# Two PSUM banks as one tile: paired exponentials and maxima, masks of two-head diagonal tiles on TensorE

## What is computed

```
h = layernorm(x) * (1 + ca) + sa
q, k, v = split(h @ w_in.T)                       # 16 heads of 16
scores = (q @ k.T) * 16 ** -0.5
scores = where(key > query, -inf, scores)         # causal
attn = softmax(scores)                            # row maximum, exp, sum
x = x + ga * ((attn @ v) @ w_out.T + b_out)
h = layernorm(x) * (1 + cb) + sb
x = x + gb * (sigmoid(xr @ W_r) * (relu(xk @ W_k) ** 2 @ W_v))   # xr, xk: h mixed with the token before
```

## Time and profile before

| | us |
|---|---|
| median of 3 runs | 1524.66 (1518.13 to 1531.08) |
| the profiled execution | 1521.95 |
| its span, first to last instruction | 1520.0 |

### The profile page before, as it was taken

The page is one execution under the profiler, slowest core; times in us unless marked ns, Lnnn a source line. Parts: engine busy times, 40 slices in busy tenths (PEclk is TensorE's granted clock), DMA queues, the critical chain, the costliest instruction groups (busy, mean ns, idle before and its releaser), DMA issues.

```text
span 1520.0 us, 28003 instructions
## 1 busy us (share of the span) xinstructions
PE 1346.2 (89%) x8744; PEld 746.3 (49%) x8744; DVE 1118.0 (74%) x3435; ACT 958.2 (63%) x1916; POOL 678.7 (45%) x1098
## 2 busy tenths in 40 slices
PE   5898889899998999889998899989998999998855
PEld 4443434455554555444554455545454555544444
DVE  8778667877678777877678777787778777777234
ACT  2167556766677666676677566776667666666633
POOL 4014122554436354553446545364546534343554
PEclk9598979999899999999899999999999898999878
DMA  4321124122331224222242223312232222221100
GB/s 139 75 64 47 42 50 112 49 65 68 84 86 46 54 66 118 67 54 55 67 108 53 56 70 97 82 44 54 72 105 63 64 54 76 68 58 50 38 29 28
DMA packets 90005, 101.77 MB, mean 67 GB/s; under 512 B 29681, under 2 KB 55545, under 8 KB 89857
## 3 DMA queue, kind: packets, MB, share of 16 engines
q1 hardware_dynamic: 89280, 99.20, 25.0%
q10 hardware_dynamic: 576, 0.79, 0.3%
HBM read 30.69 MB, written 8.94 MB: 26 GB/s over the span
## 4 chain that ended last, share of the span: by engine, by line
PE 51%; DVE 13%; SPq 10%; ACT 9%; issue 8%; POOL 7%; DMA 2%; ACTq 0%; POOLq 0%; DVEq 0%
PE val_ps L1286 13%; PE col_ps L1235 12%; PE row_ps L1264 9%; SPq L493 6%; ACT weights L815 5%; DVE row_ps L1035 5%; PE dense_ps L1296 4%; SPq L505 3%; PE dense_ps L1298 3%; PE dense_ps L1297 3%; PE dense_ps L1324 2%; DVE max_parts L1039 2%; POOL weights L664 2%; PE dense_ps L1339 2%; ACT xn_c L859 1%
## 5 line engine op out<-in xcount | busy, mean ns | idle before, releaser
L815 ACT ACTIVATE weights<-col_ps 128x512 f32<-128x512 f32 (+2 forms) x1280 | 643.7, 557 | 319.9 <-PE col_ps L1235 305.2
L1035 DVE CUSTOM_DVE_ANT_0 row_ps<-row_ps,row_mask 128x128 f32<-128x128 f32 (+3 forms) x1024 | 477.4, 517 | 209.7 <-PE row_ps L1264 209.3
L1235 PE MATMUL col_ps<-q_stack,k_stack 64*128 64x512 f32 (+3 forms) x1536 | 400.9, 410 | 36.1 <-ACT weights L815 20.4
L664 POOL TENSOR_SCALAR_AFFINE_SELECT weights<-weights 128x256 f32<-128x256 f32 x512 | 211.0, 425 | 460.1 <-ACT weights L815 458.7
L1039 DVE TENSOR_REDUCE max_parts<-row_ps 128x1 f32<-128x512 f32 x512 | 328.7, 681 | 86.5 <-PE row_ps L1264 84.8
L1286 PE MATMUL val_ps<-weights,v_ones 128*32 128x512 f32 (+3 forms) x3072 | 349.9, 529 | 25.6 <-POOL weights L664 18.1
L1264 PE MATMUL row_ps<-k_stack,q_stack 62*128 62x512 f32 (+3 forms) x1536 | 341.6, 434 | 29.3 <-DVE max_parts L1039 11.8
L1235 PEld LDWEIGHTS col_ps<-q_stack,k_stack 64*128 64x128 f32 x1536 | 210.5, 196 | 224.7 <-ACT weights L815 174.4
L1264 PEld LDWEIGHTS row_ps<-k_stack,q_stack 62*128 62x128 f32 x1536 | 163.8, 197 | 242.2 <-DVE max_parts L1035 79.9
L1035 DVE DVE_READ_ACCUMULATOR2_ANT max_parts<- 128x1 f32 x1024 | 144.7, 141 | 0.0
L1286 PEld LDWEIGHTS val_ps<-weights,v_ones 128*32 128x32 f32 x3072 | 62.1, 110 | 117.8 <-issue 61.6
(11 more groups left out here) (194 smaller groups left out, 1893.8 us busy)
## 6 DMA issues: line engine op xcount, KB each, us to landing
q_stack<-q_part SPq DMA_DIRECT2D x384, 64.0 KB, 2.2
k_stack<-k_part SPq DMA_DIRECT2D x372, 64.0 KB, 2.2
xa<-in_x SPq DMA_DIRECT2D x8, 1024.0 KB, 5.6
q_stack<-max_rows SPq DMA_DIRECT2D x512, 2.0 KB
att<-val_out SPq DMA_DIRECT2D x64, 128.0 KB
recips<-recip_rows SPq DMA_DIRECT2D x32, 256.0 KB
xq<-in_x SPq DMA_DIRECT2D x28, 256.0 KB, 3.3
out<-xq SPq DMA_DIRECT2D x28, 256.0 KB, 2.1
```

The source lines that it names most:

```text
L664: nc.gpsimd.affine_select(out=w, in_=w, compare_op=ALU.is_ge, fill=0.0, base=0, pattern=[[0, 2], [1, P]], channel_multiplier=-1).then_inc( ...
L815: nc.scalar.activation(weights[:, t % 2, heads[0]:heads[-1] + 1:2, 0:q1 - q0], col_ps[bank][:, 0:n * (q1 - q0)].rearrange("p (h q) -> p h ...
L1035: last = nc.vector.tensor_tensor_reduce(out=scores, in0=scores, in1=row_mask[:, HALF - width:HALF], scale=1.0, scalar=MASKED, op0=ALU.add, ...
L1235: last = nc.tensor.matmul(col_ps[bank][:, i * (q1 - q0):(i + 1) * (q1 - q0)], stack_at(k_stack[s % 2], rows, heads[i], P * j, P * (j + 1)) ...
```

## The change

- `col_ps` becomes one tile over both banks (`col_pair`), and `row_ps` two tiles of two banks each. One ScalarE instruction takes the exponentials of both banks of a pair and releases both at its end (`exp_done` rises by 2). 1280 instructions of one bank become 640 of two.
- One `reduce_max` takes the maxima of both banks of a pair.
- The mask of a diagonal unit with two heads a bank (128 or 256 keys) no longer is VectorE's: TensorE adds it in the bank, with eight small bf16 matmuls a pair (`mask_ident` times `mask_fill`, 128 columns and then 64), ahead of the semaphore that VectorE waits for. Units with one head a bank (384 or 512 keys) keep VectorE's custom instruction, two a pair.
- VectorE takes both early maxima of a step before it empties the dense bank; in the code before, one maximum stood before and one behind.
- The maxima are transposed by four 32 by 32 instructions in place of one of 128 by 32, into rows of 128, so that `place_max` needs two DMAs in place of eight.
- GpSimd builds the two mask constants at the start.

```diff
-PLACED = 2 * (P // SQUARE) * 16
+PLACED = 2 * 16
-        col_ps = [ps(f"col_ps{i}", [P, HALF]) for i in range(COL_BANKS)]
-        row_ps = [ps(f"row_ps{i}", [P, HALF]) for i in range(ROW_BANKS)]
+        col_pair = ps("col_ps", [P, COL_BANKS, HALF])
+        row_pair_ps = [ps(f"row_ps{i}", [P, 2, HALF]) for i in range(ROW_BANKS // 2)]
+        col_ps = [col_pair[:, i, :] for i in range(COL_BANKS)]
+        row_ps = [row_pair_ps[i // 2][:, i % 2, :] for i in range(ROW_BANKS)]
...
@@ place_max, SP
-                    for q in range(P // SQUARE):
-                        lo = SQUARE * q + 8 * MROWS * odd
-                        sp.dma_start(rows[:, :, q, :], max_rows[half][lo:lo + 8 * MROWS, :]
-                                     ).then_inc(max_placed[half], 16)
+                    sp.dma_start(stack[row:row + MROWS, half].rearrange("p g n -> p (g n)").bitcast(F32),
+                                 max_rows[half][8 * MROWS * odd:8 * MROWS * (odd + 1), :]).then_inc(max_placed[half], 16)
...
@@ exps, ACT
-                act.wait_ge(cols_ready, exp_index(b, s, c) + 1)
+                act.wait_ge(cols_ready, exp_index(b, s, c) + 2)
-                nc.scalar.activation(weights[:, t % 2, heads[0]:heads[-1] + 1:2, 0:q1 - q0],
-                                     col_ps[bank][:, 0:n * (q1 - q0)].rearrange("p (h q) -> p h q", h=n),
-                                     ACT.Exp, scale=SCALE).then_inc(exp_done, 1)
+                nc.scalar.activation(weights[:, t % 2, heads[0]:heads[0] + 2 * n, 0:q1 - q0].rearrange(
+                    "p (n o) q -> p o n q", o=2), col_pair[:, :, 0:n * (q1 - q0)].rearrange(
+                    "p o (n q) -> p o n q", n=n), ACT.Exp, scale=SCALE).then_inc(exp_done, 2)
...
@@ maximum, DVE
-                dve.wait_ge(rows_ready, at + 1)
+                dve.wait_ge(rows_ready, at + 2)
-                if k1 == P * (i + 1):
+                if k1 == P * (i + 1) and n == 1:
-                    for n in range(len(heads)):
-                        scores = bank[:, n * width:(n + 1) * width]
+                    for o in range(2):
+                        scores = banks[:, o, 0:k1 - k0]
...
-                    last = nc.vector.reduce_max(dest, bank[:, 0:len(heads) * width].rearrange(
-                        "p (h k) -> p h k", h=len(heads)), AX_X)
-                last.then_inc(max_done, 1)
+                    last = nc.vector.reduce_max(dest, banks[:, :, 0:n * (k1 - k0)].rearrange(
+                        "p o (n k) -> p o n k", n=n), AX_X)
+                last.then_inc(max_done, 2)
...
@@ split_max, DVE
-                nc.vector.transpose(max_rows[half][:], parts[:, 0:SQUARE].bitcast(F32)).then_inc(max_turned, 1)
+                for q in range(P // SQUARE):
+                    cols = slice(SQUARE * q, SQUARE * (q + 1))
+                    last = nc.vector.transpose(max_rows[half][:, cols], parts[cols, 0:SQUARE].bitcast(F32))
+                last.then_inc(max_turned, 1)
...
@@ body, DVE
                     for item in at:
                         empty_dense(*item)
-                    for u in early[1:]:
-                        maximum(b, s, u)
                     for item in at:
                         mix(*item)
-                    for u in late:
+                    for u in late[::2]:
                         maximum(b, s, u)
...
@@ row_pair, PE
+                diagonal = k1 == P * (i + 1) and len(pair[0]) == 2
-                        end = n == len(heads) - 1
+                        end = n == len(heads) - 1 and not diagonal
...
+                for n in range(len(pair[0])) if diagonal else ():
+                    for a in range(2):
+                        for odd in range(2):
+                            rows = slice(ROW_TILE * odd, ROW_TILE * (odd + 1))
+                            end = n == len(pair[0]) - 1 and a == 1
+                            last = nc.tensor.matmul(banks[odd][:, (n + 1) * width - P + ROW_TILE * a:(n + 1) * width],
+                                                    mask_ident[rows, a, :], mask_fill[rows, a, ROW_TILE * a:P],
+                                                    start=False, stop=end, skip_group_check=True)
+                            if end:
+                                last.then_inc(rows_ready, 1)
```

More of the change, by code:

```diff
@@ L160, in build @@
         max_parts = [sb(f"max_parts{i}", [P, P], F32R) for i in range(2)]
-        max_rows = [sb(f"max_rows{i}", [P, 2 * MROWS * 8]) for i in range(2)]
+        max_rows = [sb(f"max_rows{i}", [SQUARE, P]) for i in range(2)]
         val_out = [sb(f"val_out{i}", [P, HALF]) for i in range(2)]
@@ L919, in body @@
                     units = range(COL_FIRST[t], COL_FIRST[t + 1]) if attends(kind) else ()
-                    for c in units[:2]:
+                    for c in units[:1]:
                         exps(b, s, t, c)
@@ L924, in body @@
                     normalise_next(b, kind, s, t)
-                    for c in units[2:]:
+                    for c in units[2::2]:
                         exps(b, s, t, c)
@@ L1023, in maximum @@
                 at = unit_index(b, s, u)
-                bank = row_ps[bank_of(UNITS * ((s + 1) % G) + u, UNITS * G, ROW_BANKS)[0]]
-                dve.wait_ge(rows_ready, at + 1)
+                banks = row_pair_ps[bank_of(UNITS * ((s + 1) % G) + u, UNITS * G, ROW_BANKS)[0] // 2]
+                dve.wait_ge(rows_ready, at + 2)
                 i, heads, k0, k1, second = ROW_UNITS[u]
-                half, odd = i // 4, heads[0] % 2
-                col = (SPANS_AT + 16 * second + 8 * odd if half else WHOLE_AT + 16 * odd) + 4 * (heads[0] // 2) + i % 4
@@ L1029, in maximum @@
-                dest = max_parts[half][:, col:col + 4 * len(heads) - 3:4].bitcast(F32)
-                width = k1 - k0
-                if k1 == P * (i + 1):
-                    for n in range(len(heads)):
-                        scores = bank[:, n * width:(n + 1) * width]
+                half, n = i // 4, len(heads)
+                apart = 8 if half else 16
+                col = (SPANS_AT + 16 * second if half else WHOLE_AT) + 4 * (heads[0] // 2) + i % 4
+                dest = max_parts[half][:, col:col + 2 * apart].bitcast(F32).rearrange(
+                    "p (o c) -> p o c", o=2)[:, :, 0:4 * n - 3:4]
@@ L1041, in maximum @@
-                last.then_inc(max_done, 1)
[L1042 to L1045, removed]
+                            out=scores, in0=scores, in1=row_mask[:, HALF - (k1 - k0):HALF], scale=1.0, scalar=MASKED,
+                            op0=ALU.add, op1=ALU.max, accum_out=dest[:, o, :])
+                else:
+                    last = nc.vector.reduce_max(dest, banks[:, :, 0:n * (k1 - k0)].rearrange(
+                        "p o (n k) -> p o n k", n=n), AX_X)
@@ L1047, in split_max @@
+                last.then_inc(max_done, 2)
+                if u == FIRST_HALF - 2:
+                    split_max(b, s, 0, at + 2)
+                if u == UNITS - 2:
+                    split_max(b, s, 1, at + 2)
             def split_max(b, s, half, upto):
```

20 lines of the change are left out of this document (13 added, 7 removed).

## The result

The changed kernel takes 1578.72 us in the median of four executions (1563.33 to 1582.93), the kernel before 1522.78; the ratio is 1.034 (95% interval 1.026 to 1.043), so about 52 us are lost by the ratio and 56 by the medians. The profiled execution took 1575.01 us. The change is slower, as forecast, and by more than the 31 us forecast.

The account below looks back on a forecast made before the run. The prediction saw four loops through TensorE, the one from scores to exponentials tightest. Terms of 94 us lost less 62 gained made +32 us on 1522, near 1553 us; range 1488 to 1608, the forecast's own 1540 to 1580.

Parts of the forecast that it names:

- The paired exponentials: Column banks released together: ScalarE stands until both are refilled, values at t = 0 come 0.38 us later; +29 us.
- 29 + 11 - 10: Column banks released together +29 us, GpSimd's masks starting later +11, shorter exponentials where ScalarE is behind -10.
- The rival of serial banks: Column loop bounds every step of 384 or 512 columns; 93 us paid in place of 29, 1610 us; chance 0.12.
- GpSimd's masks: On the four one-pair steps GpSimd's first mask waits for the whole exponential: +11 us, bounds 0 and 45.
- Masks on TensorE: Eight matmuls for each of 128 diagonal pairs, 0.40 us a pair, 96 pairs counted: +38 us, bounds 18 and 72.
- VectorE: VectorE's work falls by a net 117 to 158 us; TensorE waits less for maxima: -34 us, bounds 0 and -80.
- SP: Two DMAs for eight land maxima 3.9 us earlier: -18 us; three more transposes on the same stretch: +8 us.
- The order: At t = 2 the dense bank is emptied behind a second custom maximum: +8 us, bounds 0 and 24.
- The signs: Observations named beforehand as showing the forecast right (exponential times, gap, VectorE busy, mask times, DMA waits) or wrong.
- Faster: Rival: VectorE is the hidden bound, its relief brings 25 us more and masks cost 18 us; 1490 us, chance 0.25.
- Nothing moves: Rival: TensorE's masks lie in waits that exist anyway and the terms cancel; 1522 us within 15, chance 0.18.

Follow-up runs that it names:

- e1: Changed kernel with exponentials taken and freed one bank at a time again, against the kernel before: 0.994, 1518 us.
- e2: Kernel before with only the paired exponentials added, one instruction over both banks: 1.026 of the kernel before, 1567 us.
- e10: Kernel before with its single-bank exponentials kept, but both banks freed only after the second: 1.018 of the kernel before, 1556 us.
- e11: Kernel before with paired exponentials only at the one-pair steps t = 2, 3, 10 and 11: 1.004 of the kernel before, 1532 us.
- e6: Changed kernel with the mask matmuls on TensorE left out, against the kernel before: 1.026, 1568 us.
- e9: Kernel before with paired maxima and the new order, all masks still on VectorE: 0.999 of the kernel before, 1527 us.
- e7: Changed kernel with exponentials by bank, one transpose and eight DMAs, against the kernel before: 0.993, 1519 us.
- e4: Changed kernel with VectorE's old order, against the kernel before: 1.042, 1592 us.
- e13: e7 with VectorE's old order, against the kernel before: 0.995, 1521 us.
- e14: e7 with all masks on TensorE, those of one-head tiles too, against the kernel before: 0.999, 1526 us.
- e12: Kernel before with 1024 small matmuls of zeros added and VectorE's masks kept: 1.001 of the kernel before, 1531 us.

## Why the prediction was right, point by point

**The paired exponentials** were the step that carried the sign, and the mechanism was right: both engines in turn at t = 0, matched by e1, e2 and e10. The size was off. The term (29 + 11 - 10 = 30 us) measured 39 alone and 62 on top of the other parts. Two things under it were too small. The first is the price at t = 0: the values come 0.57 us later and not 0.38. ScalarE's idle time before the second pair went from 0.10 to 0.68 us (medians of 32 rounds), 0.58 more where 0.48 was taken, and the first exponential starts 0.11 us later behind its matmuls; less 0.06 us saved at each of two pairs this is 0.57. The second is where it counts: 25 us at t = 0, 12 at t = 4 and 13 at t = 8 in e2, where the working has 19 us for t = 0 and 4 together and 2 for t = 8 (32 x 0.2 x 0.3). The rival of serial banks had the better picture of the gaps, which are at 219 of 256 places, but most of them cost little: its 93 us for this part are more than twice the 39.

**GpSimd's masks**: 11 us forecast; e11, which has this effect and little else, measured 5 (0 to 11), so the term may be right or twice too large.

**Masks on TensorE**: 0.40 us a pair forecast, 0.18 measured. The nearest row was the wrong neighbour: four fp32 matmuls of 128 columns take 0.28 us, eight bf16 ones take 0.18, less even than the lower bound by columns (0.28). The estimate of 0.65 us from the Trainium skill, "TensorE: Matmul & The Clock Gate", section "Back-to-back issue gap" (81 ns for a load and matmul), is further off still: here it is 22 ns, with matmuls on two halves of the array at once (the masks of the two halves start within 5 ns of each other). The prediction named a pair under 0.2 us as what would take 20 us off; e6 gives 12 us for the part and not 38, so 26 us of the sum were not there; at an equal clock it would be 24 us and 14 by the estimate above.

**VectorE**: "a net 117 to 158 us less" was wrong; the page says 21 (1118.0 to 1096.9). The term that failed is the accumulator reads. Their row says 144.7 us, and I took half as gone. But in the timeline of before a read and the next custom instruction start together:

```profile
649.56 0.14 DVE L1035 DVE_READ_ACCUMULATOR2_ANT max_parts<- 128x1 f32 x1
649.56 0.47 DVE L1035 CUSTOM_DVE_ANT_0 row_ps<-row_ps,row_mask 128x256 f32<-128x256 f32 x1
```

So they run beside each other. Counting only time that no earlier instruction covers, the 1024 reads hold VectorE 60 us and the custom maxima 427, and the change takes off 30 and 139 of these. Against that the reductions grow by 107 (1.21 us for two banks, not 1.16) and the transposes by 38; smaller groups make up the last 3. Of the 34 us of gain that were forecast for TensorE the runs show little: the load rows for maxima halved in name alone, and between e9 and e7 the move of the masks is worth 8 us in time, their cost on TensorE included. The forecast had 38 - 34 = +4 us for these two together.

**SP**: -18 us for earlier maxima, +8 for the transposes, so -10; measured +15 alone. "All go" was right of the waits, and no time came of it, since VectorE stands beside each of them, as the same sentence feared. VectorE's work for the transposes was priced right (41 us as an upper end, 38 measured); that only 0.25 us of it in 32 places would be seen, of 0.63 us in 64, was too little.

**The order**: +8 us, of a possible 24, because a wait for a maximum swallows it. Undoing it gave nothing in either kernel (e4, e13), which agrees.

**The sum.** Forecast +32, measured +52. By parts the forecast was nearer than that: 30 us for the exponentials (39 alone) and +2 for all the rest (38 + 8 + 8 - 34 - 18; -10 measured in e1), and the measured two make 29. The terms of that rest were wrong one by one, the masks dearer by 26 us than they were and VectorE's relief, by the 8 us net and the masks' 12, worth some 20 us and not 34, so that its small sum is luck. What the forecast lacked is a term for the parts together: they make 52 and not 29. By the clocks, the 23 us between have one likely source: moved to 0.922 with 9 us for 0.01, the changed kernel is 55 us slower than before, e2 is 23 and e1 19, and the sum of these two, 42, is nearer to 55. The rest of the change, which earns by its clock (0.953) when ScalarE keeps up, doesn't when the loop is serial. This last step is argued from slopes and not shown by a run of its own. That 1579 us still lies inside the forecast's own 1540 to 1580, by 1 us, is luck too.

**The signs.** Exponentials of 1.02 us, 640 of them, later values at t = 0 and no wait for `q_stack<-max_rows` came as named, and the gap came as 0.68 us where 0.5 was named. VectorE at 980 us (1097) and 0.3 to 0.5 us for the masks (0.18) did not, and of the signs of being wrong one came, the masks under 0.2 us. One reading of the profile before was too kind: 10 of the 40 slices have a clock under 0.9, so the clock was not near full "in nearly every slice".

**The rivals.** Faster: the point named was waits for maxima over 60 us now, and neither that relief (e9) nor more of it together with more masks on TensorE (e14) made the kernel faster. Nothing moves: excluded. The rules of the Trainium skill weighed in the prediction ("Perfetto Trace Analysis", sections "Matmuls" and "Optimizing Scalar/DVE Operations") spoke against the change, and e10 is the first of them measured: banks that don't alternate cost 28 us.

## What to carry to other kernels

Two banks filled and emptied in turn are worth more than the overhead that one instruction over both saves: look for a place in the timeline where the consumer runs without a gap, and price the gap as the whole way from its end to its next start (here 0.6 us against 0.06 us saved). Don't join what frees buffers where the producer has no other to fill, even if the joined engine gets less work: pairing the exponentials over both banks of `col_ps` cost 39 us, pairing the maxima over two of the four banks of `row_ps` cost nothing (e9). That the two spare banks make this difference was not tested by itself. Before adding up a row of short instructions as saved time, see in the timeline whether they run beside others; and where a comparison moves by less than 1%, look at the granted clock of each run. The versions with exponentials by bank beat both kernels, the one before by less than 1%: 1518 us or 0.994 of it in e1 (0.990 to 0.997).

## What the runs showed of the hardware

**Time follows the granted clock from run to run.** Of the kernel before, 69 executions lie between clocks of 0.906 and 0.938 and move 8.8 us for 0.01; within the other kernels with nine or ten executions the slope is 7 to 10 us. In every kept trace the granted clock is at 1.2 or at 2.4 GHz and nothing between (0.5 or 1 in these means), so the mean tells how an execution divides between the two. The kernel moves it too: small matmuls that do nothing raised it from 0.922 to 0.934 at no loss of time (e12), and leaving out the masks of the changed kernel lowered it from 0.926 to 0.912 (e6, four executions of each, which nearly touch: 0.920 and 0.918). A part that costs TensorE a little can so be free in time.

**Small bf16 matmuls on two halves of the array** are cheap: eight with their loads, of 128 and 64 columns, in 0.18 us at 2.4 GHz and 0.36 us at the least at 1.2 GHz.

**A wide ScalarE instruction over two banks** took 1.02 us where two single ones took 1.08, and started 0.09 us later behind its matmuls (0.62 and 0.53 us, e2 and e10).

**A transpose has a price of its own**: 200 ns for 32 by 32, 212 for 128 by 32.
